# Other DMA patterns for q and k rows, k buffers held across three attentions, and z copied straight to its place

## The reference

```python
# attention 1 (not causal in the softmax; masked after it, keys on and after the query)
p = softmax(q @ k.T / sqrt(2048)); p = p * triu(ones); z = p @ v   # z reshaped, added, normed
# attention 2 (causal, rotary q and k, 4 k/v heads repeated to 16)
probs = softmax(where(tril, q @ k.T * 8 ** -0.5, min)); x = x + (probs @ v) @ wo
# attention 3 (causal)
weights = softmax(q @ k.T / sqrt(128) - 1e10 * (1 - tril)); out = (weights @ v) @ ow
```

## Time and profile before

| | |
|---|---|
| Median of 3 runs | 3010.7 us |
| Profiled execution, its own time | 3020.09 us |
| Its span, first to last instruction | 3018.4 us |
| Mean granted TensorE clock | 0.875 of full speed |
| Busy: TensorE, VectorE, ScalarE, GpSimd | 84%, 66%, 47%, 13% of the span |
| DMA queue of SP and its share of 16 engines | 69640 packets, 92.05 MB, 9.0% |
| The three attentions, first k load to reciprocal | 74 to 881, 985 to 1509, 1775 to 2292 us |

### The profile page before, as it was taken

One profiled execution on the slowest core, in us unless ns is written; L12 is line 12 of the kernel. 1 busy time (PEld: TensorE's weight loads), 2 busy tenths in 40 slices (PEclk: granted clock), 3 DMA queues, 4 the chain that ended last, 5 costly groups with the idle time before them and its releaser, 6 DMA issues. The chain is left out here.

```text
span 3018.4 us, 40035 instructions
## 1 busy us (share of the span) xinstructions
PE 2528.1 (84%) x14544; PEld 1137.5 (38%) x14544; DVE 1990.5 (66%) x4005; ACT 1432.9 (47%) x2105; POOL 391.9 (13%) x562
## 2 busy tenths in 40 slices
PE   4599999999954499899669939998995989799897
PEld 2243333333321233333234414333332446443663
DVE  3788888988715688678345548867963545455453
ACT  1067676777741147547612213673682236432562
POOL 1100001000001100100100020011011323123230
PEclk7599999999986589879879966997997879898898
DMA  5000000000001100000000020000001113110320
GB/s 215 25 23 11 21 10 17 15 10 7 3 18 70 47 24 24 32 11 11 22 1 0 0 80 30 8 28 33 7 8 39 35 61 123 39 35 25 123 96 14
DMA packets 72971, 105.84 MB, mean 35 GB/s; under 512 B 23656, under 2 KB 45800, under 8 KB 71144
## 3 DMA queue, kind: packets, MB, share of 16 engines
q1 hardware_dynamic: 69640, 92.05, 9.0%
q10 hardware_dynamic: 3168, 11.64, 1.0%
HBM read 51.17 MB, written 17.17 MB: 23 GB/s over the span
## 5 line engine op out<-in xcount | busy, mean ns | idle before, releaser
L697 ACT ACTIVATE att_probs<-psum 128x1024 f32<-128x1024 f32 (+3 forms) x1152 | 1037.0, 951 | 717.9 <-PE psum L746 716.2
L655 DVE TENSOR_REDUCE att_part_max<-psum 128x1 f32<-128x512 f32 x1792 | 1128.2, 684 | 177.5 <-PE psum L728 173.8
L728 PE MATMUL psum<-att_k_rows,att_q_rows 64*128 64x512 f32 (+3 forms) x2304 | 842.0, 493 | 150.9 <-DMA att_k_rows<-att_ones 102.5
L728 PEld LDWEIGHTS psum<-att_k_rows,att_q_rows 64*128 64x128 f32 x2304 | 370.4, 200 | 812.3 <-DVE att_part_max L655 526.0
L746 PE MATMUL psum<-att_q_rows,att_k_rows 64*128 64x512 f32 (+3 forms) x2304 | 446.3, 413 | 30.5 <-DMA att_q_rows<-att_max_rows 15.1
L771 PE MATMUL psum<-att_probs,v_aug 128*9 128x512 f32 (+3 forms) x3712 | 450.1, 559 | 14.8 <-ACT att_z_sb L689 14.5
L652 DVE CUSTOM_DVE_ANT_0 att_masked<-psum,mask_max_sb 128x384 bf16<-128x384 f32 (+3 forms) x512 | 234.5, 486 | 116.5 <-PE psum L728 111.1
L746 PEld LDWEIGHTS psum<-att_q_rows,att_k_rows 64*128 64x128 f32 x2304 | 249.0, 196 | 121.1 <-ACT att_probs L697 83.4
L601 POOL TENSOR_SCALAR_AFFINE_SELECT att_probs<-att_probs 128x256 f32<-128x256 f32 x256 | 103.0, 408 | 880.4 <-ACT att_probs L697 878.2
L1352 ACT ACTIVATE latt_probs<-psum,latt_bias,latt_scale 128x192 f32<-128x192 f32 x256 | 127.5, 507 | 123.6 <-DVE latt_bias L1391 123.6
L767 PE MATMUL psum<-att_probs,att_one_only 128*9 128x512 f32 (+3 forms) x1280 | 147.6, 533 | 10.6 <-ACT att_z_sb L689 10.4
(11 more groups left out here) (258 smaller groups left out, 2608.3 us busy)
## 6 DMA issues: line engine op xcount, KB each, us to landing
att_k_rows<-k_pieces SPq DMA_DIRECT2D x48, 256.0 KB
latt_k<-local_k_T SPq DMA_DIRECT2D x32, 384.0 KB, 3.0
att_q_rows<-q_pieces SPq DMA_DIRECT2D x168, 64.0 KB
lproj_table<-in_tables SPq DMA_DIRECT2D x16, 512.0 KB, 3.6
latt_q<-local_q_T SPq DMA_DIRECT2D x32, 256.0 KB, 2.4
latt_v_own<-local_v_tok SPq DMA_DIRECT2D x32, 256.0 KB, 2.3
k_pieces<-proj_piece SPq DMA_DIRECT2D x12, 512.0 KB, 2.8
q_pieces<-proj_piece SPq DMA_DIRECT2D x12, 512.0 KB, 2.7
```

The lines of the kernel that those rows point to most:

```text
L655: nc.vector.tensor_reduce(column, ring[e % NRING][:, 0:w], AX.X, ALU.max).then_inc(ring_free, 1)
L697: nc.scalar.activation(probs[s % NPROBS][:, pr, :, at:BANK], st[pr][:, :, at:BANK], ACT.Exp, scale=scale).then_inc(st_free, 1)
L728: nc.tensor.matmul(ring[e % NRING][:, 0:w], q_rows[u % NQ][rows, pr, qt * P:(qt + 1) * P].bitcast(F32R), k_rows[g % 2][rows, pr, kc * BANK ...
```

## The change

- k in HBM is laid out so that the 16 rows of a piece follow one another (feature, then high or low), and each k load has 16 outermost rows on both sides. To store it so, each k store is two DMAs, one for each piece.
- q is loaded with its 8 features outermost and the repetition inside; so its rows in SBUF are in k's new order.
- The two `k_rows` buffers are made once and held across the three attentions. All 32 spare rows of each half are set to one, once, in `load_inputs`; the fills and the copies of ones in `attention` go.
- SP loads the k of group 1 ahead of the first maxima.
- Each unit's z is copied from SBUF to its rows of `z_T`, and its sums to their rows of `den`, by 4 + 2 DMAs; z's tensor in HBM, the reload and its wait go.

```diff
 def load_inputs(..., k_rows):
+        @block.gpsimd
+        def _(pool):
+            for i in range(2):
+                nc.gpsimd.memset(k_rows[1][64 * i + PROD:64 * i + ROWS, :, :], 1.0)
         @block.vector
+            for i in range(2):
+                nc.vector.memset(k_rows[0][64 * i + PROD:64 * i + ROWS, :, :], 1.0)
 project
+        stores_before = lambda n: 16 * sum(2 if i else 1 for m, (c, i) in enumerate(work) if m < n and m % NB == n % NB)
-                to = k_dram[:, :, chunk(c)] if i else q_dram[:, c]
-                sp.dma_start(to.rearrange("n p s -> p n s"),
-                             piece[:, n % NB, :, :]).then_inc(stored[n % NB], 16)
+                if i:
+                    for p in range(2):
+                        sp.dma_start(k_dram[:, p, :, chunk(c)], piece[:, n % NB, p, :]).then_inc(stored[n % NB], 16)
+                else:
+                    sp.dma_start(q_dram[:, c].rearrange("n p s -> p n s"), piece[:, n % NB, :, :]).then_inc(stored[n % NB], 16)
 attention
-        k_rows = [sb(f"k_rows{b}", [P, 2, S]) for b in range(2)]
-            def set_ones(b):
-                for i in range(2):
-                    row = 64 * i + PROD
-                    sp.dma_start(k_rows[b][row:row + 2, :, :].rearrange("n p s -> n (p s)"), ones[:, :]).then_inc(ones_in[b], 16)
@@ load_k
-                                     k_dram.rearrange("n (g i d p) s -> g i n d (p s)", g=NG, i=2, p=2)[g, i]).then_inc(k_in[g % 2], 16)
+                                     k_dram.rearrange("(g i d) n p s -> g i (d n) (p s)", g=NG, i=2)[g, i]).then_inc(k_in[g % 2], 16)
@@ load_q, and the same on ScalarE's queue
-                                     piece.unsqueeze(0).to_broadcast([2, HD, 2 * BANK])).then_inc(q_in[u % NQ], 16)
+                                     piece.unsqueeze(1).to_broadcast([HD, 2, 2 * BANK])).then_inc(q_in[u % NQ], 16)
@@ store_z
-                    sp.dma_start(z_dram[h * (HD + 1):(h + 1) * (HD + 1), chunk(c)], z_sb[u % 2][32 * j:32 * j + HD + 1, :]).then_inc(z_out[u % 2], 16)
+                    sp.dma_start(z_T[h * HD:(h + 1) * HD, chunk(c)], z_sb[u % 2][32 * j:32 * j + HD, :]).then_inc(z_out[u % 2], 16)
+                for a in range(2):
+                    row = 4 * g * HD + 2 * c + a
+                    sp.dma_start(den[row:row + 3 * HD + 1:HD, :], z_sb[u % 2][HD:HD + 97:32, a * PART:(a + 1) * PART]).then_inc(z_out[u % 2], 16)
@@ SP's list
             load_k(0)
-            sp.wait_ge(fill_set, 2)
-            sp.wait_ge(rows_clear, 2)
-            set_ones(0)
             load_q(2)
+            load_k(1)
             put_max(0)
             load_q(3)
+            sp.wait_ge(fill_set, 1)
             for u, (g, c) in enumerate(units):
                 if u + 1 < NU:
                     put_max(u + 1)
-                if u == 0:
-                    load_k(1)
-                    sp.wait_ge(more_clear, MORE)
-                    set_ones(1)
...
-            of_heads = z_dram.rearrange("(h r) s -> h r s", r=HD + 1)
-            for n in range(4):
-                some = slice(n * NH // 4, (n + 1) * NH // 4)
-                sp.dma_start(z_T[n * P // 4:(n + 1) * P // 4, :], of_heads[some, 0:HD, :]).then_inc(z_in, 16)
-            sp.dma_start(den, of_heads[:, HD, :].rearrange("h (a s) -> h a s", s=PART)).then_inc(z_in, 16)
-            sp.wait_ge(z_in, 16 * 5)
@@ GpSimd and VectorE
-                for b in range(1, NK):
-                    nc.gpsimd.memset(k_rows[b][spare, :, :], 0.0).then_inc(more_clear, 1)
-                nc.vector.memset(k_rows[0][spare, :, :], 0.0).then_inc(rows_clear, 1)
-            nc.vector.memset(ones[:, :], 1.0).then_inc(fill_set, 1)
@@ TensorE
-                                pe.wait_ge(rows_clear, 6)
+                                pe.wait_ge(rows_clear, 4)
-                                pe.wait_ge(ones_in[g % 2], 32)
 forward
-        k_dram = nc.dram_tensor("k_pieces", [2, P, S], F32, kind="Internal").ap()
-        z_dram = nc.dram_tensor("z_heads", [NH * (HD + 1), S], F32, kind="Internal").ap()
+        k_dram = nc.dram_tensor("k_pieces", [P // 2, 2, 2, S], F32, kind="Internal").ap()
+        k_rows = [attend.enter_context(nc.sbuf_tensor(f"k_rows{b}", [P, 2, S], F32)) for b in range(NK)]
```

More of the change, by code:

```diff
@@ L55, in bank, with load_inputs @@
     return psum[:, n * BANK:(n + wide) * BANK]
-def load_inputs(nc, psum, x, x_T, ident, loads):
+def load_inputs(nc, psum, x, x_T, ident, loads, k_rows):
     with ExitStack() as ctx:
@@ L336, in _ @@
                 sp.wait_ge(low_done, n + 1)
-                to = k_dram[:, :, chunk(c)] if i else q_dram[:, c]
-                sp.dma_start(to.rearrange("n p s -> p n s"),
-                             piece[:, n % NB, :, :]).then_inc(stored[n % NB], 16)
+                if i:
[3 more added lines that the diff above has]
+                    sp.dma_start(q_dram[:, c].rearrange("n p s -> p n s"), piece[:, n % NB, :, :]).then_inc(stored[n % NB], 16)
             for b in range(NB):
-                sp.wait_ge(stored[b], 16 * len(work[b::NB]))
+                sp.wait_ge(stored[b], stores_before(b + NB * len(work[b::NB])))
 def divide_by_sums(nc, psum, name, z_T, den, den_rows, x_T, ident, wo=None, gate=None):
@@ L448, in on_diagonal, with attention @@
         return kb // 4 == self.units[u][1]
-def attention(nc, psum, name, causal, scale, q_dram, k_dram, v_aug, z_dram, z_T, den, ident, mask=None):
+def attention(nc, psum, name, causal, scale, q_dram, k_dram, k_rows, v_aug, z_T, den, ident, mask=None):
     plan = Plan(causal)
@@ L473, in attention @@
         one_only = None if causal else sb("one_only", [P, VW])
-        ones, zeros = sb("ones", [16, BANK]), sb("zeros", [16, P])
+        zeros = sb("zeros", [16, P])
         st = [bank(psum, 2 * pr, 2).rearrange("p (i q) -> p i q", i=2) for pr in range(2)]
@@ L485, in attention @@
         more_clear = sem("more_clear")
-        ones_in = [sem(f"ones_in{b}") for b in range(2)]
         zeros_in = [sem(f"zeros_in{b}") for b in range(NQ)]
@@ L499, in attention @@
         z_free = sem("z_free")
-        z_in = sem("z_in")
-        QIN, KIN, MIN_, ZOUT = 16 * 4, 16 * 4, 16 * 2, 16 * 4
-        MORE = 2 * (NQ - 2 + NK - 1)
+        QIN, KIN, MIN_, ZOUT = 16 * 4, 16 * 4, 16 * 2, 16 * 6
+        MORE = 2 * (NQ - 2)
         diagonals = [s for s, (u, kb) in enumerate(steps) if plan.on_diagonal(u, kb)]
@@ L614, in _ @@
                 spare = slice(64 * i + PROD, 64 * i + ROWS)
-                nc.vector.memset(k_rows[0][spare, :, :], 0.0).then_inc(rows_clear, 1)
-            for i in range(2):
-                spare = slice(64 * i + PROD, 64 * i + ROWS)
                 for b in range(2):
@@ L1522, in forward @@
         first_sem = nc.free_semaphores[0]
-        load_inputs(nc, psum, a["x"], x_T, (ident, a["ident"]), [(full(b), a[n]) for n, b in early.items()])
+        load_inputs(nc, psum, a["x"], x_T, (ident, a["ident"]), [(full(b), a[n]) for n, b in early.items()], k_rows)
         with nc.Block() as block:
@@ L1543, in forward @@
                 bias=(cols["bq"], cols["bk"], early["bv0"]))
-        attention(nc, psum, "att0", False, S ** -0.5, q_dram, k_dram, v_aug, z_dram, z_T, den, ident)
+        attention(nc, psum, "att0", False, S ** -0.5, q_dram, k_dram, k_rows, v_aug, z_T, den, ident)
         divide_by_sums(nc, psum, "com0", z_T, den, den_rows, h_T, ident)
@@ L1559, in forward @@
                     rope=(w1[:, 3, :], w1[:, 4, :], angle[:, 0, :], angle[:, 1, :]))
-        attention(nc, psum, "att1", True, HD ** -0.5, q_dram, k_dram, v_aug, z_dram, z_T, den, ident, mask_max)
+        attention(nc, psum, "att1", True, HD ** -0.5, q_dram, k_dram, k_rows, v_aug, z_T, den, ident, mask_max)
         divide_by_sums(nc, psum, "com1", z_T, den, den_rows, h_T, ident, w1[:, 5, :], 1.0)
@@ L1575, in forward @@
         project(nc, psum, "proj2", h_T, w2[:, 0, :], w2[:, 1, :], w2[:, 2, :], q_dram, k_dram, v_aug)
-        attention(nc, psum, "att2", True, P ** -0.5, q_dram, k_dram, v_aug, z_dram, z_T, den, ident, mask_max)
+        attention(nc, psum, "att2", True, P ** -0.5, q_dram, k_dram, k_rows, v_aug, z_T, den, ident, mask_max)
         divide_by_sums(nc, psum, "com2", z_T, den, den_rows, x_T, ident, w2[:, 3, :], gate_of(1, 0))
```

4 lines of the change are left out of this document (2 added, 2 removed).

## The result

The changed kernel takes 2923.9 us, median of 4 runs (2920.26 to 2927.46), against 3011.4 us for the kernel before (4 runs, 3010.32 to 3013.65): ratio 0.971, 95% interval 0.969 to 0.973. 2908 us had been forecast, with 2868 to 2930 as the range. The profiled execution took 2926.28 us, span 2924.6.

The account below looks back on a forecast made before the run. TensorE was taken to be bound by waits behind DMAs, the bytes of k, q and ones setting the starts. 49.5 + 12.2 + 4 + 37.2 - 1.0 = 101.9 us off the 3010.7 median gave 2908, range 2868 to 2930.

Parts of the forecast that it names:

- Step 1: Starts of the three attentions: first issue to first matmul takes 16 us, not 32.5, at 106 GB/s; gains 49.5 us.
- rival (a): Loads flow as wide as into 128 rows and the starts reach their floor: 31 us more gained, 2877 us; 27%.
- Step 2: Second group's k issued ahead of the first maxima on SP: counted 0, range 0 to 3 us in two attentions.
- Step 3: Waits for maxima inside attentions two and three go, 12.2 us, plus 4 us from less time at low clock.
- Step 4: Ends of the three attentions: last z to reciprocal 3.7 us instead of 16.2; gains 37.2 us.
- Steps 5 and 6: Projections, each k store made two: 1.0 us lost; fills at the very start: 0.
- The base: Gain taken in full off the median 3010.7 us, 9.4 less than the profiled execution's 3020.09.
- (c): The new load patterns are no wider than before; only the ones and the ends gain: 2971 us; 4%.
- (d): SP becomes late, so TensorE waits for maxima in each of 48 units: 3053 us; 2%.
- (b): Clock and order take something back in the second and third attention: 2925 us; 12%.

Follow-up runs that it names:

- spread: Changed kernel with each 16-row load of k and q written to every second of 32 SBUF rows instead of 16 neighbours: 2902.4 us, ratio 0.962.
- order: Changed kernel with the issue of the second group's k put back behind the first unit's maxima: 2911.9 us, ratio 0.966.
- four: Changed kernel with k loaded by 16 DMAs of 4 rows, 4 rows apart, instead of 4 of 16 rows: 2921.8 us (one run).
- eight: Changed kernel with spread, order and the last copies split over two queues, k in 8 DMAs of 8 rows alternating between halves: 2918.0 us, ratio 0.966.
- narrow: Changed kernel with the loads of k and q again having two outermost rows, the rest as changed: 3003.8 us, ratio 0.996.
- narrow_order: narrow with the second group's k put back behind the first unit's maxima: 2977.3 us, ratio 0.988.
- double: Changed kernel with the third and fourth group's k loaded, waited for on SP and loaded again in each attention: 2938.8 us, ratio 0.975.
- before_again: The unchanged kernel before, run once more for a second trace: 3015.8 us (one run).

## Why the forecast was right, and where not

The time was 16 us above the forecast and within its range. Of the 101.9 us of the sum, 87.5 came by the medians, and 89.1 by the stretches that the change touches: 50.0 at the starts, 7.9 inside, 32.1 at the ends, less 0.9.

**Step 1, the starts: right in size, in part by luck.** 49.5 forecast, 50.0 measured, by a rate that few written rows set and not by the floor of rival (a). The step read the rate of 106 GB/s off the reload of z, "since few rows of SBUF are written there too". That reason doesn't hold: into two sets of 32 rows spread moves 201. The reload had 4 outermost rows and a DMA share of 0.25 (867.4 to 880.5 us of before), which points to their number as what held it; that 16 neighbouring rows give about the same rate is chance. Two errors in the working then cancel: the bytes flow at 124 GB/s and not at the 106 taken from the reload of z; and the second group's k, which the step left out of the bytes, comes in before the first matmul. Without it the start would be 14.0 us (order). Rival (a) took the rate to follow the number of outermost rows. The engines in use did: a share of 0.13 became 1.05. The rate did so only up to 4, for at 16 rows of SBUF a share of 0.34 carries nearly as much (four). The rule of the Trainium skill (SBUF — State Buffer, Door 1: The DMA port swizzle) that spoke against the change is borne out in kind. It gives 104 GB/s into 16 neighbouring partitions and 189 into 32; the runs show more, 124 and 201, with q rows and two queues in the mix. The Trainium skill (SBUF — State Buffer, Can I just issue two DMAs to hit both halves?) says that two such DMAs serialize. The 175 GB/s of eight don't contradict it, but eight changed other things too and is no proof.

**Step 2, order on SP: its zero was wrong, within its bound.** 2.38 and 1.53 us in the first trace, 1.8 in all in the second, and on the second unit's q, not on the maxima for which the step looked. It also costs 2 us at each start. The step asked the right question, what is queued ahead of whom, but only of the maxima. With narrow loads the answer would have been waits of 12 us twice (narrow).

**Step 3, waits inside: the mechanism right, the term mis-sized.** Both 6 us waits are gone, as forecast, and by the wide loads (narrow_order keeps them, double puts them back). But the term was 16.2 us with the clock, and the inner stretches of attentions two and three give 7.9 by the means of two traces each. 12.2 us of waits went. Some 2.9 came back as step 2's waits (3.9 and 1.8). Of the 4 us that the clock was to give, TensorE's busy time shows 1.3: its mean over the two attentions and two traces is 436.4 us before and 435.7 after. The remaining 2.7 us lie in pieces too small to tell from the 4 us of movement. The estimate of a gain from the clock had been read off one trace, and one attention differs by 7 us between two traces of one kernel.

**Step 4, the ends: right in kind, 5 us too large.** 37.2 forecast, 32.1 measured. The mis-sized piece is the issue: 0.67 us for a copy of z and 0.54 for one of the sums, 3.76 in all instead of 2.0, near the bound of 0.65 that the copy of ones had shown and that was taken for the range only. Landing was as forecast: 1.6 us from the last issue to the reciprocal, in the sum 1.2 and 0.4. In the units before the last the copies are hidden or cost less than can be seen.

**Steps 5 and 6** came out within the noise of the traces: +0.5 us in front of the first k issue, -0.1 between the stages. A loss of 1.0 us, as forecast, can't be told from none.

**The base.** 9.4 us were taken off for the profiled execution's distance to the median. before_again shows that the tail of that trace was 9.2 us longer than need be, mostly by the clock; its own time of 3015.78 is still 4 us above the median. So the 9.4 us were no part of what the change removes, and taking them off was right.

**Rivals.** (c), patterns no wider, is refuted by 53 against 124 GB/s. (d), SP late in each unit, did not come: SP's copies are dearer by 2.4 us per unit and TensorE waits for maxima once. (b) was the nearest by its number, 2925, but for another reason: the clock took nothing back, it only gave next to nothing. Its 474.6 and 467.3 us run to the start of the last copy of z; to its end, as it says, they are 475.24 and 467.94.

## What to carry to other kernels

Ask two questions of a slow DMA: how many engines carry it, which the DMA share of a window shows (0.13 with two outermost rows), and into which rows of SBUF it writes. The first limit hides the second. Here every second of 32 rows flowed 1.6 times as fast as 16 neighbours, and cost SP 0.5 us more for four issues (2.48 against 1.94 us at the first start). Before moving a large load ahead of a small, urgent copy, divide the queued bytes by the rate, for every waiter behind it. And trace the same kernel twice before a term is read off one stretch: here one attention moved by 7 us and unchanged code by 9, the one wholly and the other mostly with TensorE's clock.

## What the runs showed of the hardware that was not expected

- SP is held by its own DMAs when much is queued ahead of them: four 256 KB k loads take 2.28 us to issue with wide loads ahead of them and 15.39 with narrow ones.
- A copy from SBUF to SBUF of 16 KB holds SP for 0.67 us, the 18 KB store of the same rows to HBM for 0.34; three copies on ScalarE's queue take 2.2 us.
- At 16 neighbouring rows of SBUF, 124 GB/s at a DMA share of 1.05 and 118 at 0.34: a share of 1 doesn't mean that the engines are the limit.
- The granted clock differs between executions of one kernel at about the same place of its code (0.57 and 1.00 over 20 us) while TensorE is busy without a gap in both.
